# A decoder layer on one core: written-out orders for each engine, named PSUM banks, and all copies of the transposed probabilities on ScalarE

## The chip, the core and the metric

The kernel runs on one core of a Trainium2 chip. Its engines work side by side, each through its own list of instructions in order: TensorE (PE, with its weight loads as PEld), VectorE (DVE), ScalarE (ACT), GpSimd (POOL) and SyncE (SP), which issues the transfers. They wait for one another on semaphores. The metric is the device time of one execution in microseconds. The kernel before was timed three times on the chip: 417.37, 417.63 and 417.95 us, median 417.63.

## The reference

The input is x, 4 batches of 256 tokens of 256 channels. Three blocks follow each other, each with a layer norm in front and a residual behind:

```python
x = x + attn(layernorm(x), w_kv_a, q_a_gamma, w_qb, kv_a_gamma, w_kvb, w_o)   # latent attention, 16 heads, causal
x = x + xattn(layernorm(x), fside, ctx)                                       # per batch: two int8-style linears, silu(gate)*up between
x = x + ffn(layernorm(x), router_w, e_bias, W_gate, W_up, W_down, shared...)  # 32 experts, 4 per token, 40 slots each, and a shared expert
```

Attention takes softmax(q k^T / sqrt(192)) v for each head over the 256 tokens of a batch. The second block scales its inputs by column maxima, rounds both operands to whole numbers up to 127 (values are kept as floats) and multiplies; it does so twice. The router of the third block takes a sigmoid, keeps the best 3 of 8 groups and the best 4 experts in them; a token's place in an expert's 40 slots is its rank in the order of tokens, so the batches follow one another there. Everything is f32 on the outside.

## The kernel before

**Layout.** Tokens lie 128 to a tile; a batch is two tiles. Weights of the attention are folded first (step prepM): the key weights into the query weights, the value weights into the output weights. All of PSUM is one tensor of 8 banks. In the attention, banks 0 and 1 hold the scores of the even and odd heads and bank 2 the outputs; the other five take turns for everything else.

**Steps.** The program is a list of some 340 named steps, such as scores, max, exp, norm, probsT and pv of one head. A step has a part on each engine that takes part in it. For head number hn of 64 (16 heads of 4 batches):

- scores (L600, L708, L710): TensorE adds the mask and multiplies q by the keys. The score bank is used again two heads later, so TensorE waits for exp of head hn-2.
- max (L1242, L1243) on VectorE, exp (L1019, L1021) on ScalarE, norm: a reciprocal on VectorE (L1237), then GpSimd scales the probabilities (L1606, L1607).
- probsT: TensorE turns the probabilities (L609, three 128x128 turns), and a copy takes them from PSUM to SBUF: for even heads on VectorE (L1251), for odd heads on ScalarE (the helper at L960).
- pv, for two heads at once: TensorE multiplies by the values; after every second pair ScalarE copies the outputs (also L960).

Beside them run, for 4 heads of a batch at a time, q (queries), rope (VectorE L1225 and L1230, then GpSimd L1613) and qT (turn and copy); hT, fused, latents, latT, which make the latents of a later batch; y_first, y_last and y_add, the output projection of an earlier one; and, for a batch whose attention is done, the second block (steps x_stats, x_norm, x_T ... x_mm2) and the router (r_stats ... r_slots, then eight scatters on GpSimd, L1639). Each of these steps waits for the one before it, most of them through two or three engines. For the last batch they run after the attention; the shared expert (s_gate, s_up, s_silu, s_mul, s_down, s_add) is filled in there. At the end come the routed experts (xpT, gate_up, hidT, down), 20 gathers on GpSimd (L1653), and three tiles combined by matmul with a one-hot matrix (onehot L1549, mix).

**What sets the order.** plan() (L119) writes one list of steps for all engines. SLOT is the order inside one head; places holds what is put at a quarter of a head; constants (PREP_AT, FRONT_AT, Y_AT, CROSS_AND_ROUTE, FILL) say how far apart the steps of a chain stand. Names with a star stand for the other engines' part of a step when it comes later than TensorE's. From this list tensor_steps and other_steps make two: one for TensorE and one that VectorE, ScalarE and GpSimd all follow. Ring (L271) then gives banks to the steps in TensorE's order, the next of the five each time. PT_DVE = 0 (L65) sends the even heads' copies to VectorE.

Of the kernel before, what the change touches and what calls it, by code (L numbers as in the profile page):

```python
# [64 lines left out]
PT_DVE = 0  # L65
# [15 lines left out]


CROSS_AND_ROUTE = (
    ("x_stats", 0), ("x_norm", 2), ("x_T", 4), ("x_smooth", 2), ("x_scale", 1), ("x_back", 4),
    ("x_qscale", 1), ("x_round", 2), ("x_qT", 4), ("x_mm", 3), ("x_tanh", 1), ("x_gate", 1), ("x_smooth2", 2),
    ("x_scale2", 1), ("x_back2", 4), ("x_qscale2", 1), ("x_round2", 2), ("x_qT2", 4), ("x_mm2", 3),
    ("r_stats", 1), ("r_norm", 2), ("r_T", 4), ("r_logit", 3), ("r_groups", 1), ("r_best", 0),
    ("r_choose", 1), ("r_weights", 2), ("r_pos", 4), ("r_slots", 1)) + tuple((f"scatter{i}", 4) for i in range(NJ * TOPK))

SLOT = ("scores", "exp", "*pv", "*q", 0, "rope", "probsT", "max", "norm", 1, "*probsT", "qT", "pv", 2, "q", 3, "*qT")
SPLIT = ("q", "qT", "probsT", "pv", "hT", "fused", "latT", "prepM", "x_T", "x_back", "x_qT", "x_mm",
         "x_back2", "x_qT2", "x_mm2", "r_T", "r_logit")


Y_AT, WX_AT, WX_FIRST = 19, 55, 43  # L100
PREP_AT = (0, 1, 5, 7, 12, 16)
FRONT_AT, FRONT_GAPS, FRONT_NEXT = (20, 40, 54), (0, 2, 5, 8), 4

FILL = (
    ("x_stats", ("r_groups", 2)), ("x_norm", ("r_best", 2)), ("x_T", ("r_choose", 2)),
    ("x_scale", ("s_gate", 0)), ("x_scale", ("s_up", 0)), ("x_scale", ("r_weights", 2)),
    ("x_back", ("s_silu", 0)), ("x_back", ("s_mul", 0)), ("x_back", ("r_pos", 2)), ("x_qscale", ("s_down", 0)),
    ("x_qscale", ("s_gate", 1)), ("x_qscale", ("r_slots", 2)), ("x_round", ("s_silu", 1)),  # L110
    ("x_tanh", ("s_up", 1)), ("x_tanh", ("s_gate", 2)), ("x_smooth2", ("s_add", 0)), ("x_scale2", ("s_mul", 1)),
    ("x_back2", ("s_down", 1)), ("x_round2", ("s_silu", 2)), ("x_round2", ("s_add", 1)), ("x_mm2", ("s_up", 2)),
    ("r_norm", ("s_mul", 2)), ("r_logit", ("s_down", 2)), ("r_logit", ("s_gate", 3)), ("r_pos", ("s_up", 3)),
    ("r_slots", ("s_add", 2)), ("r_slots", ("s_silu", 3)), ("r_slots", ("s_down", 3)),
    ("r_slots", ("s_mul", 3)), ("r_slots", ("s_add", 3)))
SCATTER_AFTER = ("x_qscale", "x_round", "x_qT", "x_mm", "x_smooth2", "x_scale2", "x_back2", "x_qscale2")


def plan():  # L119


    places = [[] for _ in range(4 * NHU + 200)]

    def place(at, step):

        places[at].append(step)
        if step[0] in SPLIT:
            places[at + 1].append(("*" + step[0],) + step[1:])

    steps = [("setup",), ("ln1_stats", 0), ("ln1_norm", 0), ("hT", 0), ("hT", 1), ("fused", 0), ("fused", 1),  # L130
             ("latents", 0), ("prepM", 0), ("latents", 1), ("latT", 0), ("prepM", 1), ("latT", 1), ("q", 0, 0),
             ("rope", 0, 0), ("rope", 1, 0), ("qT", 0, 0), ("qT", 1, 0)]
    for p, at in zip(range(2, 8), PREP_AT):
        place(at, ("prepM", p))
    place(3, ("q", 0, 1))
    place(4, ("rope", 0, 1))
    place(6, ("qT", 0, 1))
    place(5, ("ln1_stats", 1))
    place(6, ("ln1_norm", 1))
    for b, at in zip((1, 2, 3), FRONT_AT):  # L140
        if b > 1:
            place(at - 4, ("ln1_stats", b))
            place(at - 2, ("ln1_norm", b))
        for t in (2 * b, 2 * b + 1):
            for kind, gap in zip(("hT", "fused", "latents", "latT"), FRONT_GAPS):
                place(at + gap, (kind, t))
            at += FRONT_NEXT


    units = [(NJ * b + j, c) for b in range(B) for c in range(NH // HC) for j in range(NJ)]  # L150
    ahead = 3

    def late(kind, b):

        return ("scatter", b, int(kind[7:])) if kind.startswith("scatter") else (kind, b)

    for b in range(B):
        place(4 * NH * b + (WX_AT if b else WX_FIRST), ("wx", b))
        if b == B - 1:
            break  # L160
        at = 4 * NH * (b + 1) + Y_AT
        place(at, ("y_first", 2 * b))
        place(at, ("y_last", 2 * b))
        place(at + 2, ("y_add", 2 * b))
        place(at + 4, ("y_first", 2 * b + 1))
        place(at + 4, ("y_last", 2 * b + 1))
        place(at + 5, ("y_add", 2 * b + 1))
        at += 6
        for kind, gap in CROSS_AND_ROUTE:

            at += gap if b < B - 2 else min(gap, 3)
            if b == B - 2 and kind.startswith("scatter"):
                break
            place(at, late(kind, b))

    steps += [("attention",)]
    for hn in range(NHU):
        u = hn // 2 + ahead
        for what in SLOT:
            if what in (0, 1, 2, 3):  # L180
                steps += places[4 * hn + what]
            elif what in ("scores", "max"):
                steps.append((what, hn))
            elif what in ("exp", "norm") and hn >= 1:
                steps.append((what, hn - 1))
            elif what in ("probsT", "*probsT") and hn >= 3:
                steps.append((what, hn - 3))
            elif what == "pv" and hn % 2 and hn >= 5:
                steps.append(("pv", (hn - 5) // 2))
            elif what == "*pv" and hn % 2 == 0 and hn >= 6:  # L190
                steps.append(("*pv", (hn - 6) // 2))
            elif what == "q" and hn % 4 == 2 and u < len(units):
                steps.append(("q", units[u][0] // NJ, units[u][1]))
            elif what == "*q" and hn % 4 == 3 and u < len(units):
                steps.append(("*q", units[u][0] // NJ, units[u][1]))
            elif what == "rope" and hn % 2 and u < len(units):
                steps.append(("rope",) + units[u])
            elif what in ("qT", "*qT") and hn % 2 == 0 and 2 <= hn and u <= len(units):
                steps.append((what,) + units[u - 1])
    b = B - 1  # L200

    left = [step for place in places[4 * NHU:] for step in place]
    n = left.index(("r_groups", b - 1)) if ("r_groups", b - 1) in left else 0
# [9 lines left out]
    left = left[n:]  # L213

    scatters = [("scatter", b - 1, i) for i in range(NJ * TOPK)]
    for kind, _ in CROSS_AND_ROUTE:
        steps.append(late(kind, b))
        n = SCATTER_AFTER.count(kind)
        steps += scatters[:n]
# [1516 lines left out]
```

## Time and profile before

| what | value |
|---|---|
| median of three timed runs | 417.63 us |
| the profiled execution's own time | 416.45 us |
| its span in the trace | 414.7 us |
| PE busy | 327.0 us, 79% |
| DVE, POOL, ACT busy | 233.7, 202.2, 171.7 us (56%, 49%, 41%) |
| idle of POOL before the gathers | 40.1 us, one wait |

The span is in five parts: loads and the first chain (to about 25 us), the attention with the second block and the router of three batches in it (25 to 281 us), the chain of the last batch (281 to 344 us), the experts (348 to 379 us), and the gathers (384 to 415 us). A row of the timeline gives start, duration, engine, line, operation and, in brackets, how long the engine had been idle just before and who released it. Rows of TensorE are merged where they follow one another; a matmul's end is modelled, so the distance from one start to the next says more than its duration.

### The profile page before, as it was taken

The page shows a single profiled execution, that of the slowest core. Times are in us where ns is not written, and L with a number is a line of the kernel's source. Part 1 is how long each engine was busy: PE and PEld are TensorE (multiplying, and loading weights), DVE is VectorE, ACT ScalarE, POOL GpSimd, SP SyncE. Part 2 cuts the span into 40 slices and gives each one's busy share as a digit, 9 for nine tenths or more (in the row PEclk, how much of TensorE's full clock was granted, in tenths as well). Part 3 has the DMA queues.
Part 4 walks back from the last instruction along what each step waited for, and adds up shares of the span by engine and source line. Part 5 has one row for each costly group of instructions (what it writes and reads, how often), then busy time and mean ns, then how long its engine had stood idle before and what let it go on. Part 6 is the DMA issues. An engine that isn't in the chain of part 4 may idle for free.

```text
span 414.7 us, 6650 instructions
## 1 busy us (share of the span) xinstructions
PE 327.0 (79%) x2088; PEld 227.1 (55%) x2088; DVE 233.7 (56%) x808; ACT 171.7 (41%) x552; POOL 202.2 (49%) x274
## 2 busy tenths in 40 slices
PE   3767999799999869979778969594685734997970
PEld 2344655556865547757456847473563623554860
DVE  2235556744375776965766956756946730426243
ACT  1334477576267565347366246630232100342000
POOL 1114656666475554498856379840053061000774
PEclk9989999999999999998999998998899885999995
DMA  7999900010000000000000003233005005023453
GB/s 287 402 371 314 337 1 2 0 40 1 2 0 2 2 1 2 0 13 27 7 5 2 2 1 118 80 115 115 2 3 173 1 1 134 27 77 103 102 146 107
DMA packets 18182, 32.37 MB, mean 78 GB/s; under 512 B 4185, under 2 KB 12116, under 8 KB 17508
## 3 DMA queue, kind: packets, MB, share of 16 engines
q1 hardware_dynamic: 15652, 28.70, 20.1%
q0 software_dynamic: 2496, 3.25, 3.3%
q8 instruction: 17, 0.28, 0.3%
q14 instruction: 17, 0.14, 0.1%
HBM read 26.82 MB, written 8.84 MB: 86 GB/s over the span
## 4 chain that ended last, share of the span: by engine, by line
PE 33%; DVE 26%; POOL 14%; issue 11%; ACT 8%; DMA 6%; POOLq 1%; ACTq 0%; DVEq 0%; SPq 0%
PE psum L600 24%; PE psum L609 6%; POOL expert_rows L1639 4%; DMA region_b<-expert_out,slot_gather 3%; POOL region_t L1607 2%; POOL region_t L1606 2%; PE psum L710 2%; ACT region_t L1021 1%; ACT region_r L960 1%; POOL rstd L1594 1%; DVE bn_stats L1154 1%; DVE neg_max L1243 1%; ACT region_h L960 1%; DVE q_rope_tmp L1225 1%; DVE q_chunk L1230 1%
## 5 line engine op out<-in xcount | busy, mean ns | idle before, releaser
L1607 POOL TENSOR_SCALAR region_t<-region_t,prob_rsums 128x256 f32<-128x256 f32 x64 | 59.7, 932 | 0.0
L1606 POOL TENSOR_SCALAR region_t<-region_t,prob_rsums 128x128 f32<-128x128 f32 x64 | 41.6, 650 | 26.4 <-DVE prob_rsums L1237 26.1
L600 PE MATMUL psum<-region_c,region_h 128*128 128x512 f32 (+1 forms) x128 | 47.7, 620 | 2.6 <-issue 1.8
L1653 POOL DMA_INDIRECT region_b<-expert_out,slot_gather x20 | 20.2, 1012 | 45.9 <-DMA expert_out<-region_h 40.1
L1639 POOL DMA_INDIRECT expert_rows<-h_moe,slot_scatter x32 | 33.6, 1051 | 18.4 <-DVE slot_scatter L1485 11.4
L710 PE MATMUL psum<-region_h,region_b 128*128 128x256 f32 x128 | 39.6, 392 | 0.0
L1019 ACT ACTIVATE region_t<-psum,neg_max 128x128 f32<-128x128 f32 x64 | 24.0, 376 | 35.8 <-DVE neg_max L1243 35.8
L609 PE MATMUL psum<-consts,region_t 128*128 128x128 f32 x192 | 31.9, 276 | 0.0
L600 PE MATMUL psum<-w_folded_out,region_g 128*128 128x256 f32 (+1 forms) x136 | 31.6, 384 | 0.4 <-ACT region_g L960 0.4
L1021 ACT ACTIVATE region_t<-psum,neg_max 128x256 f32<-128x256 f32 x64 | 30.9, 482 | 0.0
L600 PE MATMUL psum<-region_t,region_h 128*64 128x256 f32 (+1 forms) x256 | 28.5, 344 | 0.5 <-ACT region_t L960 0.2
L600 PEld LDWEIGHTS psum<-region_c,region_h 128*128 128x128 f32 (+1 forms) x128 | 15.7, 187 | 24.0 <-issue 21.4
L609 PEld LDWEIGHTS psum<-consts,region_t 128*128 128x128 f32 x192 | 24.7, 143 | 6.4 <-issue 0.8
L1242 DVE TENSOR_REDUCE neg_max<-psum 128x1 f32<-128x128 f32 x64 | 18.1, 283 | 16.6 <-PE psum L710 16.4
L600 PEld LDWEIGHTS psum<-w_folded_out,region_g 128*128 128x128 f32 (+1 forms) x136 | 24.7, 187 | 4.4 <-issue 0.7
L1243 DVE TENSOR_REDUCE neg_max<-psum 128x1 f32<-128x256 f32 x64 | 26.4, 413 | 0.0
L960 ACT ACTIVATE region_b<-psum 128x512 f32<-128x512 f32 x40 | 24.2, 605 | 3.9 <-PE psum L609 3.9
L708 PE MATMUL psum<-region_h,region_b 128*128 128x128 f32 x128 | 25.5, 282 | 0.0
L1613 POOL TENSOR_TENSOR q_chunk<-q_chunk,q_rope_tmp 128x256 f32<-128x256 f32 x16 | 11.7, 732 | 26.4 <-DVE q_chunk L1230 26.4
L600 PE MATMUL psum<-region_h,region_b 128*128 128x256 f32 x96 | 21.0, 380 | 2.4 <-DVE region_b L1549 2.4
L960 ACT ACTIVATE region_t<-psum 128x384 f32<-128x384 f32 x32 | 15.9, 496 | 15.3 <-PE psum L609 15.2
L600 PE MATMUL psum<-mask_bf,ident_bf 128*128 128x256 bf16 x64 | 18.2, 284 | 4.6 <-ACT region_t L1021 3.8
(212 smaller groups left out, 705.5 us busy)
## 6 DMA issues: line engine op xcount, KB each, us to landing
region_b<-in_expert_w_dram SPq DMA_DIRECT2D x10, 384.0 KB, 4.3
region_a<-in_fold_w_dram SPq DMA_DIRECT2D x3, 1152.0 KB, 9.9
region_a<-in_expert_w_dram SPq DMA_DIRECT2D x9, 384.0 KB, 10.5
expert_out<-region_h SPq DMA_DIRECT2D x8, 256.0 KB, 2.1
region_c<-in_expert_w_dram SPq DMA_DIRECT2D x5, 384.0 KB, 4.9
side_inputs<-in_expert_w_dram SPq DMA_DIRECT2D x4, 384.0 KB, 4.2
expert_rows<-region_g SPq DMA_DIRECT2D x10, 132.5 KB, 12.2
region_h<-expert_rows SPq DMA_DIRECT2D x5, 256.0 KB, 4.6
```

The costliest lines, as they stand in the source:

```text
L600: return nc.tensor.matmul(out_, lhsT, rhs, start=first, stop=last)
L609: return nc.tensor.transpose(out_, in_, ident if idn is None else idn)
L708: nc.tensor.matmul(o[:, 0:P], q[:, 0:P], kT[:, b, P:2 * P], start=False, stop=True, skip_group_check=True)
L710: nc.tensor.matmul(o[:, P:3 * P], q[:, P:2 * P], kT[:, b, :], start=False, stop=True, skip_group_check=True).then_inc(sg["scores_ready"], 1)
L960: return nc.scalar.activation(out_, in_, ACT.Copy, scale=scale)
L1019: nc.scalar.activation(probs[:, hn % 4, 0:P], s[:, 0:P], ACT.Exp, bias=nmax[:, hn, 0:1], accum_out=sums[:, hn, 0:1])
L1021: nc.scalar.activation(probs[:, hn % 4, P:3 * P], s[:, P:3 * P], ACT.Exp, bias=nmax[:, hn, 1:2], accum_out=sums[:, hn, 1:2]).then_inc(sg[" ...
L1243: v.tensor_reduce(nmax[:, hn, 1:2], s[:, P:3 * P], AX.X, ALU.max, negate=True).then_inc(sg["max_ready"], 1)
L1606: g.tensor_scalar(pr[:, 0:P], pr[:, 0:P], rsum[:, hn, 0:1], None, ALU.mult)
L1607: g.tensor_scalar(pr[:, P:3 * P], pr[:, P:3 * P], rsum[:, hn, 1:2], None, ALU.mult).then_inc(sg["probs_normed"], 1)
L1639: g.indirect_dma_start(out=xp_dram, out_offset=bass.IndirectOffsetOnAxis(ap=scat[:, NJ * b + j, k:k + 1], axis=0), in_=h3[:, b % 2, j, :], ...
L1653: g.indirect_dma_start(out=gbuf[:, n, :], out_offset=None, in_=y_dram, in_offset=bass.IndirectOffsetOnAxis(ap=gath[:, t, k:k + 1], axis=0) ...
```

## The change

plan(), its tables, tensor_steps and other_steps are gone. Instead there are four texts, one for each of TensorE, ScalarE, VectorE and GpSimd, which list the steps in the order in which that engine does them. A word is a step (letters stand for the frequent ones: s scores, m max, e exp, n norm, t probsT, v pv, r rope, u qT); the n-th time that a word comes it means the n-th step of its kind. In TensorE's text digits behind a colon name the PSUM banks that the step fills; Ring only counts how often each bank is filled and emptied. The engines' orders are now independent of one another.

The copies of probsT are all on ScalarE; VectorE's branch is taken out. Three small edits go with the new orders: the tile for the layer norm's statistics is doubled and used in turn, x_qscale of batch 0 waits until the last latT is filled, and s_silu waits until the shared expert's previous product is taken from PSUM.

```diff
-PT_DVE = 0
-SLOT = ("scores", "exp", "*pv", "*q", 0, "rope", "probsT", "max", "norm", 1, "*probsT", "qT", "pv", 2, "q", 3, "*qT")
-def plan():
...
+CODES = {"s": "scores", "m": "max", "e": "exp", "n": "norm", "t": "probsT", "v": "pv", "q": "q", "r": "rope", "u": "qT"}
+TENSOR_ORDER = """
+setup hT:0 hT:1 fused:2 fused:3 prepM:45 latT:6 prepM:70 latT:1 q:24 u:3 u:5 attention prepM:67 prepM:43 s s q:56
...
+def written(text, every_second={}):
+    taken, steps, banks = {}, [], {}
+    for word in text.split():
+        word, _, fills = word.partition(":")
+        kind = CODES.get(word, word)
+        n = taken.get(kind, 0)
+        step = steps_of(kind)[2 * n + every_second[kind] if kind in every_second else n]
+        taken[kind] = n + 1
+        steps.append(step)
+        banks[step] = [int(k) for k in fills]
+    return steps, banks
...
-                elif kind == "probsT" and a[0] % 2 != PT_DVE:
+                elif kind == "probsT":
                     hn, = a
                     wait_filled(act, step)
...
                     act.wait_ge(sg["inv_ready"], b + 1)
+                    if b == 0:
+                        wait_filled(act, ("latT", NT - 1))
...
+                u = nth(("ln1_stats", "x_stats", "r_stats")[tag], b) % 2
...
-                elif kind == "probsT":
-                    hn, = a
-                    if hn % 2 == PT_DVE:
-                        wait_filled(dve, step)
-                        if hn >= 4:
-                            dve.wait_ge(sg["heads_done"], hn // 2 - 1)
-                        empties(v.tensor_copy(probsT[:, hn % 4, :], bank(step)[:, 0:384]), step)
...
                     dve.wait_ge(sg["shared_tanh"], b + 1)
+                    if b >= 1:
+                        wait_emptied(dve, ("su", b - 1))
```

The rows below are instructions in program order, with line, operation, result and operands; line numbers differ between the two kernels.

Place 1 is TensorE in the second block of batch 0, from the turn of the rounded operands (q_bf, step x_qT) to the product that needs ScalarE's copy of it (qT_bf, step x_mm). Before:

```order
L609 MATMUL psum<-ident_bf,q_bf 128x128 x8
L600 MATMUL psum<-consts,smooth 128x128 x2
L600 MATMUL psum<-region_t,region_h 64x256 x2
L600 MATMUL psum<-region_t,region_h 64x128 x2
L600 MATMUL psum<-mask_bf,ident_bf 128x256
L708 MATMUL psum<-region_h,region_b 128x128
L710 MATMUL psum<-region_h,region_b 128x256
L600 MATMUL psum<-qT_bf 128x256 x4
```

Changed:

```order
L511 MATMUL psum<-region_c,region_h 128x512 x4
L520 MATMUL psum<-ident_bf,q_bf 128x128 x8
L511 MATMUL psum<-consts,smooth 128x128 x2
L511 MATMUL psum<-mask_bf,ident_bf 128x256
L619 MATMUL psum<-region_h,region_b 128x128
L621 MATMUL psum<-region_h,region_b 128x256
L520 MATMUL psum<-consts,region_t 128x128 x3
L511 MATMUL psum<-mask_bf,ident_bf 128x256
L619 MATMUL psum<-region_h,region_b 128x128
L621 MATMUL psum<-region_h,region_b 128x256
L511 MATMUL psum<-qT_bf 128x256 x4
```

Between the two stood one pv (region_t with region_h) and the scores of one head; now the scores of a head, a probsT and the scores of another stand there, and q (128x512) has come in front of the turn.

Place 2 is VectorE a little later, where rope of a group of heads (q_rope_tmp, region_b) stood behind the end of the second block (psum with smooth and scale_rows, step x_mm2) and the layer norm's statistics. Before:

```order
L1363 SCALAR_TENSOR_TENSOR region_r<-psum,smooth,scale_rows 128x256 x2
L1368 TENSOR_TENSOR x_residual<-x_residual,region_r 128x512
L1154 BN_STATS bn_stats<-x_residual 128x6 x2
L1156 BN_AGGR mean_var<-bn_stats 128x2 x2
L1225 TENSOR_TENSOR q_rope_tmp<-region_b,consts 128x4x2x32
L1230 TENSOR_TENSOR region_b<-region_b,consts 128x4x64
L1242 TENSOR_REDUCE neg_max<-psum 128x1
L1243 TENSOR_REDUCE neg_max<-psum 128x1
```

Changed, the same rope and what stands around it now:

```order
L1176 RECIPROCAL rden<-rden 128x3
L1139 TENSOR_TENSOR q_rope_tmp<-region_h,consts 128x4x2x32
L1144 TENSOR_TENSOR region_h<-region_h,consts 128x4x64
L1139 TENSOR_TENSOR q_rope_tmp<-region_b,consts 128x4x2x32
L1144 TENSOR_TENSOR region_b<-region_b,consts 128x4x64
L1156 TENSOR_REDUCE neg_max<-psum 128x1
L1157 TENSOR_REDUCE neg_max<-psum 128x1
```

The two ropes of a group now follow one another, and both stand ahead of the first product of the second block (x_mm), not behind its last.

Place 3 is VectorE after the attention: the two y_add (x_residual from psum), the statistics of batch 3 (bn_stats) and the router of batch 2 (scores, route, top). Before:

```order
L1163 TENSOR_SCALAR h_moe<-x_residual,mean_var,rstd 128x256 x2
L1256 TENSOR_TENSOR x_residual<-psum,x_residual 128x256 x2
L1259 MEMSET region_g 128x2x24
L1154 BN_STATS bn_stats<-x_residual 128x6 x2
L1156 BN_AGGR mean_var<-bn_stats 128x2 x2
L1384 TENSOR_SCALAR scores<-scores 128x64
L1385 RECIPROCAL scores<-scores 128x64
L1386 TENSOR_TENSOR scores<-scores,consts 128x64
```

Changed; the first y_add and the rows of scores stand ahead of these:

```order
L1308 TENSOR_TENSOR route<-route 128x16
L1314 MAX top<-route 128x8 x2
L1317 MAX_INDEX top_index<-top,route 128x8 x2
L1319 CAST top_index_f<-top_index 128x2x3
L1321 TENSOR_TENSOR route<-consts,top_index_f 128x48
L1326 TENSOR_REDUCE route<-route 128x16
L1329 TENSOR_TENSOR route<-scores,route 128x64
L1333 TENSOR_SCALAR route<-route 128x64
L1163 TENSOR_TENSOR x_residual<-psum,x_residual 128x256
L1166 MEMSET region_g 128x2x24
L1068 BN_STATS bn_stats<-x_residual 128x6 x2
L1070 BN_AGGR mean_var<-bn_stats 128x2 x2
```

Before, both y_add and the statistics came first and the router's rows then filled the waits of batch 3's chain; now the router's first two steps stand between the two y_add.

## Rows read from the trace of the kernel before

**Rows 1.** Page, part 1: busy time, share of the span, instructions

```profile
PE 327.0 (79%) x2088; PEld 227.1 (55%) x2088; DVE 233.7 (56%) x808; ACT 171.7 (41%) x552; POOL 202.2 (49%) x274
```

**Rows 2.** Windows: us, PE, PEld, DVE, ACT, POOL busy, PEclk, DMA share, GB/s

```profile
180.00:200.00 20.00, 17.46 (x115) 12.60 (x113) 13.15 (x40) 13.59 (x43) 17.70 (x21) 0.91 0.06 21
240.00:260.00 20.00, 15.81 (x112) 11.53 (x108) 12.04 (x39) 10.43 (x33) 16.94 (x21) 0.91 0.22 74
```

**Rows 3.** Timeline of PE in a stretch without waits: scores, probsT with qT, y, q

```profile
102.58 0.28 PE L600 MATMUL psum<-mask_bf,ident_bf 128*128 128x256 bf16 x1
103.36 0.49 PE L609 MATMUL psum<-consts,region_t 128*128 128x128 f32 x3
104.12 3.62 PE L600 MATMUL psum<-w_folded_out,region_g 128*128 128x256 f32 x16
107.58 0.27 PE L600 MATMUL psum<-mask_bf,ident_bf 128*128 128x256 bf16 x1
...
114.66 2.94 PE L600 MATMUL psum<-region_c,region_h 128*128 128x512 f32 x8
117.53 0.28 PE L600 MATMUL psum<-mask_bf,ident_bf 128*128 128x256 bf16 x1
```

**Rows 4.** Timeline, 25 to 62 us: waits of PE, and DVE before the second

```profile
25.20 0.37 PE L600 MATMUL psum<-mask_bf,ident_bf 128*128 128x256 bf16 x1 [0.78 <-ACT region_b L960]
...
38.78 0.73 DVE L1163 TENSOR_SCALAR region_r<-x_residual,mean_var,rstd 128x256 f32<-128x256 f32 x2 [1.47 <-POOL rstd L1594]
...
39.95 3.02 PE L600 MATMUL psum<-region_c,region_h 128*128 128x512 f32 x8 [1.83 <-issue]
...
61.22 0.33 PE L609 MATMUL psum<-consts,region_r 128*128 128x128 f32 x1 [0.30 <-DVE region_h L1209]
```

**Rows 5.** Timeline, 62 to 157 us: the first and the last wait of PE

```profile
66.15 0.44 PE L609 MATMUL psum<-consts,region_r 128*128 128x128 f32 x2 [0.81 <-DVE region_r L1163]
...
155.47 0.66 PE L609 MATMUL psum<-consts,region_b 128*128 128x128 f32 x4 [1.99 <-POOL region_b L1613]
```

**Rows 6.** Timeline, 157 to 231 us: the first and the last wait of PE

```profile
185.59 1.12 PE L609 MATMUL psum<-consts,x_scaledT 128*128 128x128 f32 x4 [2.09 <-ACT x_scaledT L960]
...
218.92 0.66 PE L609 MATMUL psum<-consts,region_b 128*128 128x128 f32 x4 [1.73 <-POOL region_b L1613]
```

**Rows 7.** Timeline, 231 to 282 us: the first and the last wait of PE

```profile
248.86 0.66 PE L609 MATMUL psum<-consts,x_scaledT 128*128 128x128 f32 x4 [3.14 <-ACT x_scaledT L960]
...
281.18 0.66 PE L600 MATMUL psum<-small_weights,h_moeT 128*64 128x32 f32 x16 [0.73 <-issue]
```

**Rows 8.** Groups by line and form: copies, exp, scores' first matmul, a scaling

```profile
L1251 DVE COPY region_t<-psum 128x384 f32<-128x384 f32 x32 | 17.4, 542 | 1.4 <-PE psum L609 1.3
L960 ACT ACTIVATE region_t<-psum 128x384 f32<-128x384 f32 x32 | 15.9, 496 | 15.3 <-PE psum L609 15.2
L1019 ACT ACTIVATE region_t<-psum,neg_max 128x128 f32<-128x128 f32 x64 | 24.0, 376 | 35.8 <-DVE neg_max L1243 35.8
L600 PE MATMUL psum<-mask_bf,ident_bf 128*128 128x256 bf16 x64 | 18.2, 284 | 4.6 <-ACT region_t L1021 3.8 <-ACT region_b L960 0.8
L960 ACT ACTIVATE region_r<-psum,smooth 128x256 f32<-128x256 f32 x16 | 6.3, 475 | 9.4 <-DVE smooth L1308 9.4
```

**Rows 9.** Timeline, the chain of the last batch: where it begins, and ScalarE's second scaling

```profile
279.57 0.87 PE L600 MATMUL psum<-region_t,region_h 128*64 128x256 f32 x8 [0.24 <-ACT region_t L960]
...
283.80 0.42 DVE L1256 TENSOR_TENSOR x_residual<-psum,x_residual 128x256 f32<-128x256 f32 x1 [0.44 <-PE psum L600]
...
309.90 0.51 ACT L960 ACTIVATE x_scaledT<-region_r,smooth 128x256 f32<-128x256 f32 x1
```

**Rows 10.** Timeline, the end: the one-hot product, the first and the last of 20 gathers

```profile
380.60 20.99 PE L600 MATMUL psum<-region_h,region_b 128*128 128x256 f32 x96 [2.36 <-DVE region_b L1549]
383.75 1.06 POOL L1653 DMA_INDIRECT region_b<-expert_out,slot_gather  x1 [40.09 <-DMA expert_out<-region_h]
...
408.78 1.00 POOL L1653 DMA_INDIRECT region_b<-expert_out,slot_gather  x1 [0.30 <-issue]
```

More of the change, by code:

```diff
@@ L78 @@
 SLOTS_A, SLOTS_B, SLOTS_C = 9, 10, 5
[L83 to L88, printed above, removed]
@@ L95 @@
-SLOT = ("scores", "exp", "*pv", "*q", 0, "rope", "probsT", "max", "norm", 1, "*probsT", "qT", "pv", 2, "q", 3, "*qT")
[L96 to L115, printed above, removed]
@@ new lines @@
+x_mm:4 v s t:6 s v t:3 s x_back2:5 t:4 v t:7 t:6 x_qT2:34 y_first:5 t:7 x_mm2:6 t:3 v y_first:4 v r_T:7 y_last
+r_logit:6 y_last s_gate:3 s_up:7 tail s_gate:0 s_up:1 r_pos:2 x_T:5 s_gate:6 x_back:42 s_down:5 s_up:3 x_qT:70
+s_down:4 x_mm:5 s_down:2 x_back2:1 x_qT2:63 x_mm2:7 r_T:0 r_logit:4 r_pos:5 s_gate:2 s_up:1 s_down:6 xpT:3 xpT:7
+gate_up:0 gate_up:4 hidT:5 gate_up:2 down:1 hidT:6 xpT:3 xpT:7 xpT:0 hidT:5 down:4 gate_up:2 gate_up:1 down:6 hidT:3
+gate_up:7 hidT:0 gate_up:5 down:4 down:2 hidT:1 gate_up:6 hidT:3 down:0 down:7 hidT:5 down:4 mix:2 mix:1 mix:3
@@ new lines @@
+r r prepM m m wx n n prepM m m n n r r m m n n m prepM n prepM m n latents r r m ln1_norm m n n m m latents n n m wx
+m n n r r r r m m n n r m r m n m n m n n r m r m n ln1_norm n y_add m m n n latents m n y_add x_stats latents m
+x_norm m n x_T latents x_smooth m n latents n r r m n x_back m x_round n wx r r m m x_mm n n x_gate m n x_smooth2
+x_back2 r r x_round2 m m n x_mm2 r_stats m n r_norm n r m r m n r_groups r_best m r_choose y_add r_weights y_add
+x_stats n x_norm r x_T m r n x_smooth m m n x_back n m x_round r_slots n m x_mm n x_gate n r x_smooth2 r m x_back2 m
@@ new lines @@
+n wx x_round2 m n m x_mm2 n r_stats m n r_norm r r m n r_groups n r_best r_choose r_weights r_slots m y_add m n
+y_add x_stats n m x_norm m n n x_T r r x_smooth m m x_back n n m m x_round n m x_mm n x_gate m n m n x_smooth2 m
+x_back2 n n x_round2 x_mm2 r_stats r_norm y_add r_groups r_best y_add x_stats r_choose x_norm r_weights x_T r_slots
+x_smooth s_silu s_mul x_back s_silu s_add s_mul x_round s_silu s_mul s_add x_mm x_gate s_add x_smooth2 x_back2
+x_round2 x_mm2 r_stats r_norm r_groups r_best r_choose r_weights r_slots s_silu s_mul s_add xpT gate_up slot_weights
@@ new lines, in written @@
+def written(text, every_second={}):
[9 more added lines that the diff above has]
+    return steps, banks
+ITEMS = {
+    "hT": ("hT",), "fused": ("fused",), "latT": ("latT",),
+    "prepM": ("prepM", "mo",),
+    "qT": ("qT",), "probsT": ("probsT",), "y_first": ("y",),
+    "x_T": ("xT",), "x_back": ("xs", "ws",), "x_qT": ("xqT", "xb",),
+    "x_mm": ("h1",), "x_back2": ("as",), "x_qT2": ("aqT", "wb",), "x_mm2": ("h2",),
+    "r_T": ("h3T",), "r_logit": ("logit",), "r_pos": ("pos",),
+    "s_gate": ("sg",), "s_up": ("su",), "s_down": ("sd",),
+    "xpT": ("xpT",), "gate_up": ("gu",), "hidT": ("hidT",), "down": ("dn",),
+    "mix": ("mix",),
```

238 lines of the change are left out of this document (83 added, 155 removed), and 3 rows, old and new, of the table ITEMS.

## The prediction, made before the changed kernel was run

> **What bounds the kernel now.** I read the busy line of the page first: TensorE works for 327.0 of 414.7 us and no other engine for more than 56% [rows 1]. So the question is what makes TensorE wait, and where. Then the windows, to part the stages: the start (to 25 us) and the end (from 384 us) move data, the chain of the last batch (281 to 344 us) is one dependence after another, and from 25 to 281 us TensorE is the engine that is nearly full. Then TensorE's timeline through these 256 us, reading only the rows with a bracket. It has 33 waits: 5 up to 62 us, 0.78, 0.47, 1.83, 0.37 and 0.30, together 3.75 us [rows 4]; 13 up to 157 us, from 0.81 to 1.99, together 9.65 us [rows 5]; 7 up to 231 us, together 7.82 us [rows 6]; 8 up to 282 us, together 9.56 us [rows 7]. All in all 30.8 us. The releasers are many: GpSimd's rope, ScalarE's copies, exp, a layer norm. So no engine's speed is short; a step stands in a queue where its input is not there yet, or the input's maker stands behind something longer. Two of the waits go with a lower clock: the 20 us around 185.59 and around 248.86 have a granted clock of 0.91 [rows 2].
>
> **Part 1: the copies.** VectorE loses 32 copies of 542 ns, 17.4 us; ScalarE gets 32 of 496 ns, 15.9 us [rows 8]. VectorE's gain is on the path nowhere in the attention as a sum, since it is 56% busy. ScalarE's 15.9 us are covered by its own idle time: before exp alone it waits 35.8 us for the maxima [rows 8]. If that cover were gone all 15.9 us would be paid. I take 0 for the part by itself; bounds -3 (rope and the maxima come sooner) and +15.9.
>
> The Trainium skill (Perfetto Trace Analysis, Optimizing Scalar/DVE Operations) says that shifting work from VectorE to ScalarE may make sense when VectorE is saturated; at 56% it is not, so by that rule this part is worth nothing, and if the orders are worth nothing too the time stays at 417.6. [...]
>
> **Part 2: the orders in the attention.** I walked TensorE's new list by hand with start-to-start times of the trace: scores of a head 0.78 us, probsT and qT in front of y 0.76 together, y of a tile 3.46, q of a group 2.87 [rows 3], and set the other engines' steps beside it with their durations and about 0.05 us for each hand-over. What is left of the waits:
>
> - Up to 62 us. The 1.83 us before q come from a copy on VectorE (L1214) that stood behind a normalisation, which waited 1.47 us for GpSimd [rows 4]. The statistics and that normalisation now stand before the first max, and two prepM now fill the 0.78 us before the first scores. At the ninth scores the walk is 2.7 us ahead. Left: 1.0 of 3.75.
> - To 157 us. The last wait, 1.99, is qT behind rope, and rope stood behind x_mm2 and the statistics on VectorE; now it stands in front of x_mm (place 2), some 10 us earlier in the list. The 0.99 us before x_mm (qT_bf) had one pv and one head's scores as cover, about 1.6 us; now two heads and a probsT, about 2 us (place 1). The latents of batches 2 and 3 are one long block earlier than needed. In this walk almost no wait comes up. Left: 1.5 of 9.65.
> - To 231 us. From y_first of batch 1 on, the walk of 40 us finds 0.6 before x_back, 0.55 before x_qT, 0.2, 1.1 before x_back2 (VectorE does one rope before x_smooth2, and ScalarE copies q ahead of x_scale2), 0.25, 0.2. Left: 3.5 of 7.82.
> - To 282 us there is little other work for TensorE. The walk finds 1.4 us before the scores of head 60, since exp of head 58 is queued on ScalarE behind x_qscale (4 of 475 ns, [rows 8]), 1.05 before head 62, 0.95 before a pv that waits for the copies of head 59, 1.0 before x_qT2, and smaller ones: 6.2. Left: 6.5 of 9.56.
>
> Recovered: 30.8 - 12.5 = 18.3 us. No wait of 2 us is left, so the lower clock of the two windows should go: 9% of 2 x 20 us at full speed are 3.6 us, its highest value; 0 is the lowest; I take 1.8. Against it: the walk sees neither a bank that is not yet empty nor a queue's small delays. If what I recover is everywhere only the share of the last stretch (3.06 of 9.56, a third), 9.9 are recovered, not 18.3. So what it misses lies between 0 and 8.4; I take 4.
>
> **Part 3: the chain of the last batch.** Count from the end of the last pv, 279.57 + 0.87 = 280.44. Before, the second y_add starts at 283.80, 3.4 us later, and ScalarE's second scaling (x_scale2) at 309.90, 29.5 us later [rows 9]. Now r_groups and r_best of batch 2 stand between the two y_add (place 3), so batch 3's statistics start some 3.3 us later; its chain then meets fewer of the router's rows on VectorE, but s_silu, s_mul and s_add of batches 1 and 2 now stand ahead of x_mm and x_smooth2, and four products of the shared expert ahead of x_T on TensorE. Walked in the same way, x_scale2 comes 31.0 us after the pv. From there to the scatters the chain is as before. Cost: +1.5 us (bounds -1.5 and +5). On GpSimd the power for x_smooth2 now stands behind all eight scatters of batch 2, not four; they should be done some 4 us before it is wanted.
>
> **Part 4: experts and end.** TensorE's order of gate_up, hidT and down is shuffled, and the 16 one-hot rows stand earlier. The product that waited 2.36 us for them starts sooner. But the end is set by the 20 gathers, 1.32 us from one start to the next (25.03 us over 19), 26 us from the last store of expert rows on [rows 10]; the product takes 21 us beside them. So 0 (bounds -0.7 and +1). The three small edits cost 0: what they wait for stands ahead in the same engine's queue anyway.
>
> **Sum.** -18.3 - 1.8 + 4 + 1.5 = -14.6. The profiled execution took 416.45 us, 414.7 of them span; 416.45 - 14.6 = 401.85. The median of the timed runs is 1.18 above it: **403.0 us**. With the bounds of the waits alone, 403.0 - 5.8 to 403.0 + 6.2.
>
> **Rivals.**
> - Most waits come back elsewhere (a cross-attention block is one chain, whatever stands beside it). For it: the last stretch of the walk. Against it: the waits up to 157 us have plain causes that are gone. A third recovered, no gain of clock: 416.45 - 9.9 + 1.5 = 408.05, as a median 409.2.
> - The walk misses nothing and the clock stays up: 416.45 - 18.3 - 3.6 + 1.5 = 396.05, as a median 397.2.
> - ScalarE in order decides. A copy that waits for its turn stands ahead of an exp, and with two score banks TensorE's next scores wait for that exp; 3.8 us of TensorE's waits before scores name exp already [rows 8]. If each of the 32 copies delays its exp by its 496 ns, 15.9 us come on top of the third recovered: 408.05 + 15.9 = 423.95, as a median 425. It decides from 0.26 us a copy on (8.4 / 32). Against it: ScalarE was idle before exp for 35.8 us, and the new text mostly puts a probsT copy right behind an exp.
> - The orders recover just what the moved copies cost: no change, 417.6.
>
> **How the numbers follow.** Forecast 0.64; a third recovered 0.14; nothing missed 0.12; no change 0.04; ScalarE decides 0.06. Less than 0.2% (0.8 us) can't be told from no change here. Faster: 0.64 + 0.14 + 0.12 = 0.90; same 0.04; slower 0.06. The range goes from 395, below the second rival, to 414, above the first with a tail that costs its 5 us: 2 in 10 are left out, the cases of 0.04 and 0.06 and the rest beyond either end.
>
> **What the profile would show.** Right: TensorE's bracketed waits from its first scores to the end of the last pv add up to 13 to 17 us; that pv ends near 264; the wait of qT for rope and the waits at the layer norms are gone; the windows there have a clock of 1.00; ScalarE is near 188 us busy and VectorE near 216; x_scale2 of the last batch comes about 31 us after the last pv. Wrong: waits of scores for exp that grow to more than 10 us in all (ScalarE), x_scale2 more than 34 us after the pv (the chain), waits of TensorE for a bank, or a later first gather for the same end of the chain.

## The result, and the profile after

After took 391.64 us (median of 4 runs, 389.62 to 394.15), before 417.79 beside it on the same chip (417.37 to 418.0): a ratio of 0.938, 95% interval 0.932 to 0.944, so 26.2 us less. Forecast was 403.0 us, in a range of 395 to 414: the direction was right, the time lies 11 us under the forecast and 3 under the range.

The two profiled executions took 416.45 and 389.62 us; that of after is the fastest of its four. The first view is the page of after, its busy lines and its slices:

```profile
PE 316.7 (82%) x2088; PEld 222.0 (57%) x2088; DVE 229.2 (59%) x776; ACT 183.8 (47%) x584; POOL 203.2 (52%) x274
...
PE   2869999999999999999998988996722709998940
...
PEclk9999999999999999999999999999965776999995
```

Beside [rows 1], TensorE makes the same 2088 matmuls in 10.3 us less; ScalarE has 12.1 us more. VectorE has 4.5 us less, not 17: some of its other instructions took longer (the last section). The slices of TensorE are 80% full or more from 29 us to the last pv, and its clock does not fall before the tail.

Next, who let TensorE wait in the attention (engine, line waited for: us in total, times, longest us; 25 to 252 us, the seven largest):

```profile
PE psum L520 <- POOL region_t L1515: 2.3, 5, 1.0
PE psum L511 <- ACT region_t L932: 1.6, 3, 1.1
PE psum L511 <- DVE chosen L1351: 1.0, 1, 1.0
PE psum L520 <- ACT x_scaledT L871: 0.8, 2, 0.6
PE psum L520 <- POOL region_b L1521: 0.7, 2, 0.4
PE psum L511 <- ACT region_t L871: 0.7, 1, 0.7
PE psum L520 <- DVE q_bf L1263: 0.6, 2, 0.3
```

The waits for x_scaledT (2.09 us in [rows 6], 3.14 in [rows 7]) are down to 0.8 us in two, and the 1.99 us for rope [rows 5] are gone. Read wait by wait, as the prediction did for before, TensorE now stands for 9.2 us: 0.7 to 62 us, 1.1 in the next stage, 3.3 in that of [rows 6] and 4.1 in the last. Both sums hold one wait behind the last pv (0.73 us before, 0.18 after); up to the last pv it is 30.0 and 9.0. Then the chain of the last batch in the timeline, the last pv, the second addition of y and ScalarE's second scaling:

```profile
251.49 0.87 PE L511 MATMUL psum<-region_t,region_h 128*64 128x256 f32 x8
...
259.14 0.42 DVE L1163 TENSOR_TENSOR x_residual<-psum,x_residual 128x256 f32<-128x256 f32 x1
...
281.92 0.51 ACT L871 ACTIVATE x_scaledT<-region_r,smooth 128x256 f32<-128x256 f32 x1 [2.64 <-DVE smooth L1245]
```

The last pv ends at 252.36, 28.1 us before that of [rows 9]; the addition comes 6.8 us behind it (3.4 before), the scaling 29.6 us (29.5 before). At the other end, the gathers (min/median/max ns, first and last start) run as in [rows 10]:

```profile
L1561 POOL DMA_INDIRECT region_b<-expert_out,slot_gather x20: 994/998/1140, 356.7 to 381.9; - x20
```

Last, the clock. In before and then in after, four microseconds each (us, TensorE busy, its granted clock, share of DMA, GB/s):

```profile
24.00:28.00 4.00, 3.22 (x27) 0.63 1.01 410
...
184.00:188.00 4.00, 2.42 (x12) 0.68 0.10 36
188.00:192.00 4.00, 4.00 (x18) 0.89 0.11 39
248.00:252.00 4.00, 3.14 (x21) 0.79 0.01 4
252.00:256.00 4.00, 3.15 (x23) 0.79 0.17 46
```

```profile
24.00:28.00 4.00, 4.00 (x55) 1.00 1.00 404
...
184.00:188.00 4.00, 3.43 (x28) 1.00 0.07 21
188.00:192.00 4.00, 3.74 (x36) 1.00 0.11 33
248.00:252.00 4.00, 4.00 (x26) 1.00 0.00 0
```

Before has three stretches at half clock (1.2 in place of 2.4 GHz), each behind a sparse one; the prediction had looked at two. Busy time times the missing clock, summed over windows of 1 us from 24 us to the last pv, is 4.9 us in before (1.6, 1.5 and 1.7) and 0.0 in after. The first of the three is no gain that one can count on: nine profiles of kernels that begin as after does, all those of experiments 2 to 4, 6, 7 and 9 to 12, have a granted clock of 0.50 to 0.75 from 24 to 28 us, and only the profile of after has 1.00.

So the 27.0 us between the spans of the two profiles (414.7 and 387.7) are: TensorE's waits up to the last pv, 30.0 - 9.0 = 21.1 before rounding; clock 4.9; 0.6 for the router's turns of batch 2, which now stand behind the last pv; about 1.4 that I can't place; less 1.0 us from the last pv to the first scatter (53.2 before, 54.2 after). From there on the kernels agree within 0.2 us.

### The profile page after: what moved, and what is told of

It reads as the page before. It is cut to its first block, busy times and chain, and to the rows that moved or that the text cites. A ratio compares the mean times of both kernels' runs of the same rounds, so it can differ in the third digit from the quotient of the medians.

```text
span 387.7 us, 6657 instructions
## 1 busy us (share of the span) xinstructions
PE 316.7 (82%) x2088; PEld 222.0 (57%) x2088; DVE 229.2 (59%) x776; ACT 183.8 (47%) x584; POOL 203.2 (52%) x274
## 4 chain that ended last, share of the span: by engine, by line
PE 48%; DVE 19%; POOL 12%; issue 10%; DMA 7%; ACT 3%; POOLq 1%; DVEq 0%; ACTq 0%; SPq 0%
PE psum L511 30%; PE psum L520 11%; PE psum L621 4%; DMA region_b<-expert_out,slot_gather 3%; POOL expert_rows L1547 3%; PE psum L619 2%; POOL region_t L1515 2%; POOL region_t L1514 1%; POOL region_b L1561 1%; ACT region_r L871 1%; DMA expert_out<-region_h 1%; DVE bn_stats L1068 1%; DVE q_rope_tmp L1139 1%; DVE q_chunk L1144 1%; POOL rstd L1502 1%
## 5 line engine op out<-in xcount | busy, mean ns | idle before, releaser
L1515 POOL TENSOR_SCALAR region_t<-region_t,prob_rsums 128x256 f32<-128x256 f32 x64 | 62.1, 970 | 0.0
L1514 POOL TENSOR_SCALAR region_t<-region_t,prob_rsums 128x128 f32<-128x128 f32 x64 | 39.7, 621 | 23.7 <-DVE prob_rsums L1151 23.0
L1547 POOL DMA_INDIRECT expert_rows<-h_moe,slot_scatter x32 | 32.8, 1024 | 15.2 <-DVE slot_scatter L1392 8.0
L871 ACT ACTIVATE region_t<-psum 128x384 f32<-128x384 f32 x64 | 31.3, 505 | 14.8 <-PE psum L520 14.7
L621 PE MATMUL psum<-region_h,region_b 128*128 128x256 f32 x128 | 38.2, 381 | 0.0
L930 ACT ACTIVATE region_t<-psum,neg_max 128x128 f32<-128x128 f32 x64 | 24.0, 375 | 22.2 <-DVE neg_max L1157 20.4
L932 ACT ACTIVATE region_t<-psum,neg_max 128x256 f32<-128x256 f32 x64 | 30.7, 480 | 0.0
L520 PEld LDWEIGHTS psum<-consts,region_t 128*128 128x128 f32 x192 | 21.8, 141 | 13.0 <-POOL region_t L1515 6.0
L871 ACT ACTIVATE region_b<-psum 128x512 f32<-128x512 f32 x40 | 22.6, 604 | 10.2 <-PE psum L520 10.1
L1473 DVE SCALAR_TENSOR_TENSOR x_residual<-region_b,token_weights,x_residual 128x256 f32<-128x256 f32 x20 | 9.7, 484 | 26.9 <-DMA region_b<-expert_out,slot_gather 26.9
L511 PEld LDWEIGHTS psum<-region_t,region_h 128*64 128x64 f32 x256 | 15.7, 136 | 14.1 <-issue 8.9
L1501 POOL TENSOR_SCALAR var_eps<-mean_var 128x2 f32<-128x2 f32 x12 | 2.8, 235 | 36.9 <-DVE mean_var L1070 36.9
```

The costliest lines, as they stand in the source:

```text
L511: return nc.tensor.matmul(out_, lhsT, rhs, start=first, stop=last)
L520: return nc.tensor.transpose(out_, in_, ident if idn is None else idn)
L621: nc.tensor.matmul(o[:, P:3 * P], q[:, P:2 * P], kT[:, b, :], start=False, stop=True, skip_group_check=True).then_inc(sg["scores_ready"], 1)
L871: return nc.scalar.activation(out_, in_, ACT.Copy, scale=scale)
L930: nc.scalar.activation(probs[:, hn % 4, 0:P], s[:, 0:P], ACT.Exp, bias=nmax[:, hn, 0:1], accum_out=sums[:, hn, 0:1])
L932: nc.scalar.activation(probs[:, hn % 4, P:3 * P], s[:, P:3 * P], ACT.Exp, bias=nmax[:, hn, 1:2], accum_out=sums[:, hn, 1:2]).then_inc(sg[" ...
```

## The experiments

Before ran beside each of them; ratios are to it. The theories: the orders remove TensorE's waits (T-order); the fuller TensorE keeps its clock (T-clock). Against them, that relieving VectorE of the copies (T-copies) or the banks (T-banks) do it.

**1. The copies alone.** In before: `PT_DVE = 0` becomes `PT_DVE = 2`.

> The kernel before with one thing of the change alone: ScalarE takes all 64 copies of the transposed probabilities, VectorE none; orders and rotating banks stay. If the gain comes from the orders (T-order), this is worth about nothing or loses: 32 copies x 0.50 us = 16 us more on ScalarE, whose in-order line already delays exps (35.8 us of waits); 415 to 433 us, likeliest 420, with TensorE's waits at 30 us or more. If relieving VectorE is what brings the gain (T-copies), VectorE is 32 x 0.542 = 17.3 us shorter and the time falls by 5 us or more, to 412 or less.

414.19 us, ratio 0.993 (0.990 to 0.995): 3.1 us faster. Neither expectation: not a loss, not the whole. TensorE's waits up to the last pv are 26.0 us (30.0 in before). Exp's wait for the maxima falls from the 35.8 us of [rows 8]:

```profile
L1019 ACT ACTIVATE region_t<-psum,neg_max 128x128 f32<-128x128 f32 x64 | 24.3, 379 | 24.8 <-DVE neg_max L1243 24.8
```

**2. Half the copies back in the new order.** In after, 32 words `t` go from ScalarE's text to VectorE's, and VectorE gets the copy of before:

```diff
-m n n r r r r m m n n r m r m n m n m n n r m r m n ln1_norm n y_add m m n n latents m n y_add x_stats latents m
+n n m wx m t n t n r r r r m m n n r m t r m n m n m t n n r m r m t n ln1_norm n y_add t m m n n latents m n y_add t
```

> The kernel after, with the copies of the even heads back on VectorE, each put where VectorE stood at the time at which ScalarE made it in the trace of after; all else as after. T-order: the waits of TensorE in the attention stay near 9 us, time 388 to 397. T-copies: half of the gain or more goes, 400 us or more, since VectorE is 17 us busier and the maxima come late.

411.43 us, 0.987 (0.984 to 0.990). T-order failed here: 20 of the 26 us are gone with the new order still in place. The waits of VectorE say how (first its copies, then, as a group, ScalarE's exp):

```profile
DVE region_t L1164 <- PE psum L520: 19.7, 13, 3.2
```

```profile
L930 ACT ACTIVATE region_t<-psum,neg_max 128x128 f32<-128x128 f32 x64 | 23.9, 373 | 40.3 <-DVE neg_max L1157 38.7
```

Up to 252 us VectorE stood 19.7 us in 13 waits for turns that TensorE had not made yet (24.9 in 15 up to the last pv), the maxima behind them came late, and exp waited 38.7 us for them (20.4 in after). TensorE's own waits up to the last pv are 22.9 us again; the longest are not for exp (2.0 us) but for other steps behind VectorE's queue, as GpSimd's part of rope (6.3) and the second block's norm (3.9). That may be my placing, so:

**3. The same copies, later.** 24 of the 32 words `t` move to just before the maximum of the next scores.

> As the run with half the copies back on VectorE (411.4 us, where VectorE stood 19.7 us in 13 waits for the turns that it was to copy), but 24 of the 32 copies now stand right before the maximum of the scores that TensorE makes next behind the turn, so that VectorE need not wait for the turn; the other 8 are where they were. If the loss there was my placing (T-order), the time falls to 389 to 397. If VectorE's line has no place for them that suits both the maxima and the products (T-copies), it stays above 400.

406.50 us, 0.971 (0.966 to 0.976). VectorE's waits at the copies fell to 7.5 us, but TensorE now waited 7.0 us, in six waits, for these copies, and 19.7 us in all up to the last pv. By the ratios that is 14 us over after, by the medians 15: T-copies by its own number. Both placings stand in an order that was written for copies on ScalarE; an order written anew for shared copies was not tried.

**4. The load without the tie.** After, unchanged, but at those 32 places VectorE does something nobody waits for:

```diff
+                elif kind == "probsT":
+                    v.tensor_reduce(sm[:, a[0] // 2 % 4, 31 + a[0] // 8 % 5:32 + a[0] // 8 % 5], cst[:, 0:384], AX.X, ALU.max)
```

> The kernel after, all copies still on ScalarE, but VectorE makes 32 reductions of 128x384 numbers that nobody waits for (some 0.55 us each by the rows of 256 and 512 numbers, the length of a copy), at the 32 places at which the run with the copies put later (406.5 us) had them. If VectorE's 17 us more of work cost the 15 us there (T-load), the time is 402 to 408 again. If it was the tie (VectorE stands until the turn is made, and the product until VectorE comes to the copy: T-tie), it stays at 391 to 396.

399.55 us, 0.956 (0.949 to 0.963), between the two: 8 of the 14 to 15 us come with VectorE's time alone. The rest I put down to the tie of the copy to the turn and the product; experiment 3 also takes 32 copies off ScalarE, so this is argued, not shown. The reductions took 540 ns each (17.3 us in all):

```profile
L1161 DVE TENSOR_REDUCE smooth<-consts x32: 519/540/547, 39.0 to 251.1; 128x1 f32<-128x384 f32 x32
```

TensorE's waits up to the last pv rank the four kernels as their times do: 9.0 us in after (391.6), 13.9 here (399.6), 19.7 in experiment 3 (406.5), 22.9 in experiment 2 (411.4). So does exp's wait for the maxima (20.4, 27.1, 34.5 and 38.7), a sign of how late VectorE's queue runs; it is no measure by itself, since experiment 1 has 24.8 us at 414.2. VectorE was 59% busy in after. The Trainium skill (Perfetto Trace Analysis, Optimizing Scalar/DVE Operations) has it that offloading may make sense where VectorE is saturated; here VectorE was far from that, and taking the copies from it was still worth 14 to 15 us in the new order; the measurement decides.

**5. The banks alone.** Before's orders and copies, in after's text, with the bank that was given free first named for each tile, as here in TensorE's text:

```diff
+... q:23 u:4 u:5 attention s prepM:67 prepM:34 q:56 s prepM:73 u:4 prepM:56 s u:3 q:74 s prepM:56 t:3 s ...
```

> The orders and the split of the copies of the kernel before, but each PSUM tile named a bank: the one of the five (eight outside the attention) that was given free first in the order of the program, in place of the next in rotation; 219 of 272 tiles change their bank. T-order: the matmuls wait for steps that are late, not for banks: within 2 us of before, 415.5 to 419.5. If the banks themselves are the gain (T-banks): 10 us or more off, 407 or less.

417.48 us, 1.002 (0.999 to 1.004): no change. Its waits are before's (8.2 us in 5 for x_scaledT, the longest 3.1). The names bring nothing by themselves; whether the new order could run with rotating banks was not tried.

**6. Two waits put back.** After, with the turn of x_scaledT earlier on TensorE in batches 1 and 2:

```diff
-... x_T:7 s t:5 v t:4 s s x_back:63 v ... x_T:7 t:5 s v t:4 s u:6 u:3 x_back:57 v ...
+... x_T:7 s t:5 v x_back:63 t:4 s s v ... x_T:7 t:5 s v x_back:57 t:4 s u:6 u:3 v ...
```

> The kernel after, with the turn back of the scaled x of batches 1 and 2 moved two to four steps earlier on TensorE, right behind a head pair's product, where each meets a wait of about 2.3 us as in before. Order alone: 2 x 2.3 us less what the later steps gain, 393 to 396, clock 1.00 throughout. With T-clock: a stretch of half clock behind each wait, 2 x 1.7 us more, 396 to 400, and granted clock of 0.91 in the 20 us that hold each.

397.11 us, 0.951 (0.946 to 0.955): 5.5 us over after, for two steps that were moved. The timeline has the two waits, and the windows behind them have a clock of 1.00:

```profile
174.06 0.66 PE L520 MATMUL psum<-consts,x_scaledT 128*128 128x128 f32 x4 [2.24 <-ACT x_scaledT L871]
...
228.77 0.66 PE L520 MATMUL psum<-consts,x_scaledT 128*128 128x128 f32 x4 [2.30 <-ACT x_scaledT L871]
```

```profile
172.00:176.00 4.00, 1.94 (x16) 1.00 0.00 0
176.00:180.00 4.00, 3.82 (x30) 1.00 0.02 4
228.00:232.00 4.00, 3.23 (x26) 1.00 0.01 0
232.00:236.00 4.00, 2.66 (x21) 1.00 0.79 250
```

The waits cost their 4.5 us without any help of the clock: T-order, and not the T-clock of my expectation. All in all TensorE waits 13.9 us up to the last pv, 9.0 in after.

**7. The same waits, longer.** Two reductions of 0.54 us on VectorE ahead of each scaling.

```diff
+                    for i in range(2 if b in (1, 2) else 0):
+                        v.tensor_reduce(sm[:, b, 31 + i:32 + i], cst[:, 0:384], AX.X, ALU.max)
```

> The run with two waits of 2.3 us back (397.11 us, clock at 1.00 behind both), with two reductions of 0.54 us more on VectorE ahead of each of the two scalings that TensorE waits for, so that the waits are 3.4 us, longer than the 3.14 us behind which before showed half clock. Order alone: 2 x 1.1 us more, 398.5 to 400, clock at 1.00 in the attention. T-clock, with the length of the wait as what decides: a stretch of half clock behind each, 1.6 us each on top: 401.5 to 403.5.

399.76 us, 0.957 (0.954 to 0.960). The waits became 2.92 and 3.21 us. Behind the first the clock stayed, behind the second it fell, and 1.7 us of matmul time went (busy time by missing clock, in windows of 1 us from 230 to 235 us). So of the 2.7 us over experiment 6, 1.6 are wait, and the fall bears the rest:

```profile
174.36 0.66 PE L520 MATMUL psum<-consts,x_scaledT 128*128 128x128 f32 x4 [2.92 <-ACT x_scaledT L871]
...
230.01 0.66 PE L520 MATMUL psum<-consts,x_scaledT 128*128 128x128 f32 x4 [3.21 <-ACT x_scaledT L871]
```

```profile
176.00:180.00 4.00, 4.00 (x32) 1.00 0.02 4
228.00:232.00 4.00, 1.99 (x13) 0.85 0.01 0
232.00:236.00 4.00, 3.54 (x21) 0.72 0.10 17
```

**8. Before with its holes filled.** The fold products of pair 2 ahead of the first scores, and dummy transposes ahead of the wait for x_scaledT of batches 1 and 2:

```diff
+DUMMY = {1: 8, 2: 15}
...
+                            if b in DUMMY:
+                                wait_empty(pe, item)
+                                for i in range(DUMMY[b]):
+                                    turn(bank(item)[:, 0:P], ident)
                             wait_emptied(pe, ("xT", b))
```

> The kernel before, with its three waits ahead of the stretches of low clock filled: the fold products of pair 2 stand ahead of the first scores (as in after), and 8 and 15 transposes of the identity, written over by the real ones, stand ahead of the wait for x_scaledT of batches 1 and 2 (waits of 2.09 and 3.14 us). T-clock: TensorE's clock stays at 1.00 in the windows 25:45, 185:205 and 245:265 (0.91 before), and 3 x 1.7 us of matmul time come back: 412 to 414.5. If the waits rather than the clock cost the time, the clock may rise but the time stays within 1 us of before (416.5 to 418.5).

412.63 us, 0.987 (0.982 to 0.993): the time that T-clock asked for, but not for its reason. The low stretches only moved (to 24, 204 and 255 us); the clock's loss to the last pv is 4.5 us against 4.9, and the last pv ends 0.8 us earlier. The rest lies behind it (1.7 us up to the first scatter, 1.4 from the first turn of the expert rows to the first gather), and I can't say why. Inconclusive.

**9. Before's order behind the attention.** After, with the four engines' words behind the last head pair in before's order.

> The kernel after, with the order of before behind the last head pair (last y products, cross and shared MLP, routing of batches 2 and 3), up to the first transposes of the expert rows. From the last pv to the first scatter before took 53.18 us and after 54.22. If the order there is the cause of the 1.0 us, this takes it back: about 1 us under after, 389 to 392 with the stretch at 53.2. If the low clock there (0.81 against 0.90) is the cause, the stretch stays at 54 to 55 and the time within 1 us of after.

391.26 us, 0.937 (0.933 to 0.941), no change; from the last pv to the first scatter 54.6 us. So the old order is not worth more in the time. What costs the 1.0 us between the two profiles stays open, since the granted clock in that stretch differs as well: 0.90 in before, 0.81 in after, 0.84 here.

**10. A better order there.** In that stretch VectorE still has routing of batch 2 to do, and in after it stands between the steps of batch 3. I set the chain of batch 3 first and let the rest fill its gaps, worked out with durations of the trace. VectorE's piece:

```diff
-x_back2 n n x_round2 x_mm2 r_stats r_norm y_add r_groups r_best y_add x_stats r_choose x_norm r_weights x_T r_slots
+r_stats r_norm y_add y_add x_stats r_groups x_norm x_T x_smooth r_best x_back r_choose x_round s_silu r_weights x_mm
```

> The kernel after, with a new order on the four engines behind the last head pair alone: the two additions of y and the layer norm of batch 3 first, the routing steps of batch 2 and the shared MLP only in the gaps of the chain of batch 3. Worked out from the durations of the trace of after, the last pv to the first scatter of batch 3 falls from 54.2 to 48 us: time 384 to 387. If the chain there is bound by TensorE at its low clock (0.81) instead, it gains under 2 us: 389.5 or more.

385.55 us, 0.923 (0.919 to 0.928): 6 us under after, faster than both. The stretch is 48.6 us (253.40 to 302.03):

```profile
252.53 0.87 PE L511 MATMUL psum<-region_t,region_h 128*64 128x256 f32 x8
...
302.03 0.98 POOL L1547 DMA_INDIRECT expert_rows<-h_moe,slot_scatter  x1 [0.78 <-POOL h_moe L1539]
```

**11. Its waits filled.** Transposes of the identity into the bank of the step that waits:

```diff
+DUMMY = {("r_pos", 2): ("pos", 22), ("x_back2", 3): ("as", 9), ("x_qT2", 3): ("aqT", 17), ("r_pos", 3): ("pos", 28),
+         ("xpT", 0): ("xpT", 60)}
...
+                if step in DUMMY:
+                    name, n = DUMMY[step]
+                    wait_empty(pe, (name,) + a)
+                    for i in range(n):
+                        turn(bank((name,) + a)[:, 0:P], ident)
```

> The reordered tail (385.55 us) with TensorE's waits behind the attention filled: 22, 9, 17 and 28 transposes of the identity in the waits of 3.7, 1.8, 2.8 and 4.6 us, and 60 in the 9 us before the first expert rows arrive; each is written into the bank of the step that waits. T-clock: the matmuls behind them run at full clock; by the rows at half speed (two bf16 turn groups, two rows of scales, two products, and the first 4 us of the experts) 1.5 + 1.9 us come back: 381.5 to 383.5. If the clock falls there all the same or the fillers run over, 385 to 388.

384.40 us, 0.918 (0.912 to 0.924), not to be told from experiment 10. Up to the scatter the clock rose from 0.80 to 0.96 (first row experiment 10, second this one), and the stretch lost only 0.9 us:

```profile
253.40:302.03 48.63, 33.81 (x191) 0.80 0.19 62
```

```profile
255.28:303.05 47.77, 38.47 (x273) 0.96 0.19 64
```

The 60 transposes ended 3.6 us before the rows came, and the clock fell again:

```profile
306.62 6.71 PE L523 MATMUL psum<-consts 128*128 128x128 f32 x60
316.96 1.11 PE L523 MATMUL psum<-consts,region_h 128*128 128x128 f32 x4 [3.63 <-DMA region_h<-expert_rows]
```

**12. The last wait filled to its end.** `("xpT", 60)` becomes `("xpT", 88)`.

> The reordered and filled tail (384.4 us, where the last of the 60 transposes ended 3.6 us before the expert rows came, and the clock was at half again for the first 4 us of the experts), with 88 transposes there in place of 60: they last until some 0.5 us before the rows. T-clock: the experts start at full clock, half of 4 us comes back: 382 to 383. If the start of the experts is bound by something else (their weights, the rows), 384 to 385 with the clock up.

379.61 us, 0.908 (0.906 to 0.910), the fastest: 12 us under after, 4 to 5 under experiment 11. Here T-clock is shown for a part of it. The wait before the rows is 0.67 us, and from the last pv to the end of the experts the clock is 1.00:

```profile
304.81 9.77 PE L523 MATMUL psum<-consts 128*128 128x128 f32 x88
315.25 1.40 PE L523 MATMUL psum<-consts,region_h 128*128 128x128 f32 x8 [0.67 <-DMA region_h<-expert_rows]
```

```profile
254.00:301.00 47.00, 36.73 (x273) 1.00 0.20 65
301.00:315.00 14.00, 13.58 (x104) 1.00 0.13 33
315.00:347.00 32.00, 30.32 (x241) 1.00 0.32 96
```

From the first turn of the expert rows to the end of the last down product it is 28.2 us here, and 31.3 in experiment 11, 29.5 in experiment 10, 30.2 in after, whose experts start at half clock; busy time by missing clock is 0.0, 3.1, 1.8 and 2.6 us there. From that end to the first gather it is 3.7 us here and 5.7 to 5.9 in these three. This part is not the clock's: experiment 8 has 3.7 us there too, with experts that start at half clock.

## Why the prediction was wrong

**What the walk misses, +4: the step that failed first.** The walk left 12.5 us of waits; 9.2 came. It missed nothing of weight; it was too careful by 3.3 us, and the term on top, chosen between 0 and 8.4, by another 4: together 7.3 of the 12.2 us by which the sum is off (401.85 forecast for the profiled execution, 389.62 measured). The doubt for which I added it (banks that are not empty) was tested by experiment 5 from the other side: banks were no limit in before either. Stage by stage the walk left 1.0, 1.5, 3.5 and 6.5 us, and 0.7, 1.1, 3.3 and 4.1 were measured: good, and too high only in the last, where the waits behind ScalarE's queue were shorter.

**The clock, -1.8: too small.** I took half of the highest value, 3.6 us for two windows; measured are 3.3 us in these two, all of it back, so the term was too small by about 1.5. The profiled pair shows 1.6 us more, from the third stretch around 26 us (the wait ahead of it is in [rows 4]), which makes 3.1 us in that pair. This part is an accident of the execution: the runs of after had spans of 387.7, 388.6, 390.5 and 392.2 us at mean clocks of 0.947, 0.942, 0.930 and 0.926, and experiment 6, with the instructions of after up to 170 us, shows the low stretch at the start that the profile of after lacks:

```profile
24.00:28.00 4.00, 4.00 (x47) 0.64 1.00 403
```

**The copies, 0: not a term by itself.** With the old order they were worth 3.1 us (at my bound of -3), with the new one 14 to 20 (experiments 1 to 4). So neither the orders nor the copies bring the gain alone. My walk had them on ScalarE, so the sum is not off by them, but its reason is: I argued from ScalarE's idle time and VectorE's 56%, where the experiments point to how late the steps behind the copies in VectorE's queue come. The rival in which ScalarE's queue decides is refuted: waits of scores for exp (L932) are 1.6 us, 3.8 before [rows 8].

**The tail, +1.5: right in size in the profiled pair, wrong in place.** The scaling was forecast 31.0 us behind the last pv and came at 29.6; 1.0 us was lost up to the scatter. But 54.2 us is the least: in experiments 2, 3, 4, 6 and 7, which have the order of after there, this stretch took 56.1 to 56.9 us at a granted clock of 0.73 to 0.76, so the cost may be up to 3.8 us. Whether the order or the clock bears it is not shown: experiment 9 changed nothing in the time, and in another order experiment 11 raised the clock to 0.96 for 0.9 us only.

**Experts and end, 0:** 30.95 us from the first gather to the end before, 31.03 after. Right.

Put together for the profiled execution: 401.85 - 4 - 3.3 - 3.1 - 0.5 = 390.95, against 389.62 measured; the rest is the router's turns and what I can't place. The nearest rival was the one in which nothing is missed and the clock stays up (397.2, given 0.12); it still kept the walk's 12.5 us, and 3.6 us for the clock.

## What to carry over

Where several in-order queues feed one full engine, walk the new order by hand with durations of the trace and believe the walk (here 12.5 us of waits walked, 9.2 measured); a lump for what it may miss has to be bounded by something seen. Price a copy that is moved by what stands behind it in the old queue, not by how busy either engine is, and try it in the new order as well as in the old. Take the clock from several executions before you count it. And look for low clock in every stretch of the program in small windows: the same walk, turned on the last batch's chain, and a filled wait ahead of the experts gave another 12 us.

## What the runs showed of the hardware

- Waits of 2.24, 2.30 and 2.92 us in an otherwise busy TensorE left the clock at 1.00; behind 3.21, 3.14 and 3.63 us it fell to half, and in before also behind 2.09 us. So the length of a wait alone doesn't decide, and the same first instructions ran at 1.00 in one profile and at 0.50 to 0.75 in nine others: one profile can lack a fall that others have.
- Dummy transposes held the clock at 1.00 through 9.8 us in which TensorE had nothing else to do (experiment 12); filling three holes in before moved the low stretches elsewhere (experiment 8).
- A clock of 0.96 in place of 0.80 in a chain of short steps came with 0.9 us less of 48; in the dense experts a full clock was worth 1.4 to 3.1 us of 28 to 31.
- VectorE's product with the cosines took 482 ns a time in one of rope's three buffers before and 794 ns after, the same instruction on the same data (first before, then after; busy us, mean ns, idle before). Why wasn't tried; it is 2.4 of the 12.9 us that VectorE did not get back from the copies, and the same product in another buffer (q_chunk, 451 and 564 ns) is 1.8 more.

```profile
L1230 DVE TENSOR_TENSOR region_b<-region_b,consts 128x256 f32<-128x256 f32 x8 | 3.9, 482 | 0.0
```

```profile
L1144 DVE TENSOR_TENSOR region_b<-region_b,consts 128x256 f32<-128x256 f32 x8 | 6.3, 794 | 0.0
```
